# Adding word numbers on TensorE and making the list of neighbour words with five wide VectorE operations

## What is computed

```python
def layer0(X, adj):                       # X 8192x128, adj 8192x8192
    mask = adj != 0
    vals = max over j of (X[j, :] where mask[i, j])      # for each row i
    return where(any(mask, axis=1), vals, 0)

x = layernorm(x + layer0(x, adj))
x = layernorm(x + L1(x, W1, a1, adj))     # thresholded attention
x = layernorm(x + L2(adj, x, W2, a2))     # attention
x = layernorm(x + L3(x, adj, W3, a3))     # attention
```

## Time and profile before

| | us |
|---|---|
| timed, median of 3 | 4908.3 |
| profiled execution, span from first to last instruction | 5439.8 |
| neighbour maximum in the profile, about | 0 to 2222 |
| three attention layers in the profile, about | 2222 to 5440 |

### The profile page before, as it was taken

The page is one execution under the profiler, slowest core; times in us unless marked ns, Lnnn a source line. Parts: engine busy times, 40 slices in busy tenths (PEclk is TensorE's granted clock), DMA queues, the critical chain, the costliest instruction groups (busy, mean ns, idle before and its releaser), DMA issues. The chain is left out here.

```text
span 5439.8 us, 68010 instructions
## 1 busy us (share of the span) xinstructions
PE 4559.6 (84%) x22263; PEld 2172.7 (40%) x22263; DVE 4311.2 (79%) x7371; ACT 2207.6 (41%) x2430; POOL 1205.9 (22%) x1342
## 2 busy tenths in 40 slices
PE   4766776677667766579999999999999999999999
PEld 3333333333333333323443333454444445444444
DVE  6666676667666667788888888889999987999998
ACT  3444444444444444398888888410000001000000
POOL 5555445454444455200000000000000000000000
PEclk6888888888888889889999999999999999999999
DMA  7555555555555555233232332122222202212220
GB/s 272 195 187 184 192 197 185 187 182 194 186 179 188 193 169 166 95 130 122 105 126 111 113 127 105 64 102 83 75 84 79 81 9 99 102 70 98 76 96 14
DMA packets 181695, 709.72 MB, mean 130 GB/s; under 512 B 31168, under 2 KB 39872, under 8 KB 132224
## 3 DMA queue, kind: packets, MB, share of 16 engines
q1 hardware_dynamic: 110816, 566.01, 29.3%
q0 software_dynamic: 33760, 73.21, 4.2%
q10 hardware_dynamic: 36864, 67.13, 3.5%
HBM read 630.59 MB, written 79.82 MB: 131 GB/s over the span
## 5 line engine op out<-in xcount | busy, mean ns | idle before, releaser
L1750 PE MATMUL bank<-w,GX 128*128 128x512 f32 x4096 | 1768.4, 593 | 4.8 <-DVE w L1865 4.8
L1865 DVE SCALAR_TENSOR_TENSOR w<-q,E,m 128x512 f32<-128x512 f32 x2048 | 1472.1, 758 | 130.8 <-PE bank L1750 39.1
L356 POOL DMA_INDIRECT ring<-x_ext,idx x1051 | 1032.8, 983 | 1074.2 <-DVE X L619 316.8
L1750 PEld LDWEIGHTS bank<-w,GX 128*128 128x128 f32 x4096 | 777.7, 191 | 975.3 <-issue 975.2
L607 DVE TENSOR_TENSOR top<-top,sums 128x1024 f32<-128x1024 f32 x484 | 589.2, 1217 | 626.7 <-remote 364.8
L507 PE MATMUL sums<-lone,xs 128*128 128x512 fp8e4 x3000 | 838.3, 421 | 287.0 <-DVE top L607 214.9
L1200 PE MATMUL acc<-w,GX 128*128 128x512 f32 x2048 | 939.6, 605 | 65.8 <-DVE w L1458 62.6
L430 ACT ACTIVATE stage<-tp 128x1024 fp8e4<-128x1024 uint16 x512 | 523.7, 1025 | 1088.1 <-remote 598.3
L1458 DVE SCALAR_TENSOR_TENSOR w<-q,E,u 128x1024 f32<-128x1024 f32 x512 | 634.7, 1274 | 1.9 <-PE acc L1200 1.8
L507 PEld LDWEIGHTS sums<-lone,xs 128*128 128x128 bf16 x3000 | 291.5, 105 | 814.7 <-issue 607.4
L1200 PEld LDWEIGHTS acc<-w,GX 128*128 128x128 f32 x2048 | 371.9, 190 | 564.5 <-issue 413.5
(11 more groups left out here) (250 smaller groups left out, 2919.3 us busy)
## 6 DMA issues: line engine op xcount, KB each, us to landing
adjb<-in_adj SPq DMA_DIRECT2D x256, 1024.0 KB
m<-mask_t SPq DMA_DIRECT2D x128, 1024.0 KB, 4.8
mask_t<-stage ACTq DMA_DIRECT2D x256, 256.0 KB
den_m<-mask_t SPq DMA_DIRECT2D x64, 1024.0 KB, 6.9
keep_m<-mask_t SPq DMA_DIRECT2D x64, 1024.0 KB, 4.9
ring<-x_ext,idx POOLq DMA_INDIRECT x1051
z<-row_scores SPq DMA_DIRECT2D x30, 256.0 KB, 4.6
xt_rows<-XT SPq DMA_DIRECT2D x8, 512.0 KB, 4.7
```

The lines of the kernel that those rows point to most:

```text
L356: pool.indirect_dma_start(ring[:, s, :], None, x_ext, bass.IndirectOffsetOnAxis(ap=idx[:, k, s:s + 1], axis=0)).then_inc(done, 16)
L1750: last = nc.tensor.matmul(acc[b][:, :], GX[:, j, :], w[:, j % WR, :], start=(j == 0), stop=(j == T - 1))
L1865: nc.vector.scalar_tensor_tensor(out=w[:, j % WR, :], in0=q, scalar=E[:, j:j + 1], in1=m[:, b, j, :], op0=ALU.max, op1=ALU.mult).then_inc( ...
```

## The change

TensorE no longer starts the tally with the first count. Before the counts of blocks 0 and 4 one matmul of 512 columns (`one_row` x `numbers`) writes word numbers times 2^-7 into a whole bank of the tally, and the counts add to it. So each code carries its number (0 to 255, within its half of the row) in its lowest bits. `before` is scaled up to 2^20. VectorE then makes: the exponents of the codes (one source, no mask), codes less exponents, the number put into the exponents of words that don't open a group, and the minimum of these with `before`, by which words without an earlier one drop out. That minimum now signals `cnt_used`. The largest eight are taken of each half of `codes`, so `many` has 16 entries; the peeled ones take the places of the 64 words that open a group in `keys`. ScalarE's mask is gone. New constants are made at the start, for which TensorE waits.

```diff
-MORE = 8
+LEAST = 2.0
+HALVES = 2
+HW = NW // HALVES
+NUMBER = 2.0 ** -7
+BEFORE = 2.0 ** 20
+MORE = 8 * HALVES
...
-                if 1 <= t <= T:
-                    act.wait_ge(counted, t)
-                    nc.scalar.activation(opens[:, :, 1:WPG], before, ACT.Relu, bias=top_bit[:, 0:1], scale=-TOP_BIT).then_inc(opens_made, 1)
...
+            word_steps.did(nc.gpsimd.iota(half_no[:, :, :], pattern=[[HW, HALVES], [0, 8]], base=0, channel_multiplier=0))
+            word_steps.do(nc.gpsimd.memset(one_row_f, 0.0))
+            word_steps.do(nc.gpsimd.affine_select(out=one_row_f, in_=one_row_f, compare_op=ALU.not_equal, fill=1.0, base=0, pattern=[[0, P]], channel_multiplier=1))
...
             pe.wait_ge(again, 5)
+            pe.wait_ge(numbers_made, 1)
...
             def count(q, k, e):
 
+                if e % (T // TRB // HALVES) == 0:
+                    bank = slice(e * TRB, e * TRB + T // HALVES)
+                    nc.tensor.matmul(tally[:, bank, :].rearrange("p t c -> p (t c)"), one_row[:, :], numbers[:, :, :].rearrange("p t c -> p (t c)"),
+                                     start=True, stop=False, skip_group_check=True)
                 for g in range(e * TRB, (e + 1) * TRB):
-                    last = nc.tensor.matmul(tally[:, g, :], stage[:, q, g, k * P:(k + 1) * P], powers[:, :], start=True, stop=True)
+                    last = nc.tensor.matmul(tally[:, g, :], stage[:, q, g, k * P:(k + 1) * P], powers[:, :], start=False, stop=True, skip_group_check=True)
...
-                    hold(dve, opens_made, s + 1)
-                    steps.did(nc.vector.tensor_tensor(out=bits(by_group(high)), in0=bits(code_ps), in1=bits(opens[:, :, :]), op=ALU.bitwise_and))
+                    steps.did(nc.vector.tensor_scalar(bits(keys[:, :, :]), bits(code_ps), EXPONENT, None, ALU.bitwise_and))
...
-                    nc.vector.tensor_tensor(out=by_group(x), in0=code_ps, in1=by_group(high), op=ALU.subtract).then_inc(cnt_used, 1)
+                    steps.did(nc.vector.tensor_tensor(out=by_group(x), in0=code_ps, in1=keys[:, :, :], op=ALU.subtract))
+                    steps.settle()
+                    side.did(nc.vector.tensor_tensor(out=bits(not_opening), in0=bits(not_opening), in1=by_group(code_no[:, :])[:, :, 1:WPG], op=ALU.bitwise_or))
                 if finishes:
                     into(old, 0, 2).then_inc(lower_free, 1)
                 if extracts:
-                    hold(dve, cnt_used, s + 2)
-                    steps.do(nc.vector.tensor_scalar(bits(high), bits(x), EXPONENT, None, ALU.bitwise_and))
-                    steps.did(nc.vector.tensor_tensor(out=x, in0=x, in1=high, op=ALU.subtract))
+                    steps.settle()
+                    side.settle()
+                    nc.vector.tensor_tensor(out=not_opening, in0=not_opening, in1=before, op=ALU.min).then_inc(cnt_used, 1)
                 step(2)
                 if extracts:
-                    steps.settle()
-                    steps.did(nc.vector.tensor_tensor(out=bits(x), in0=bits(x), in1=code_no[:, :], op=ALU.bitwise_or))
-                    side.did(nc.vector.tensor_tensor(out=bits(high), in0=bits(high), in1=code_no[:, :], op=ALU.bitwise_or))
-                    steps.settle()
-                    steps.did(nc.vector.max(out=y, in_=x))
+                    for a in range(HALVES):
+                        steps.did(nc.vector.max(out=y[:, 8 * a:8 * a + 8], in_=x[:, a * HW:(a + 1) * HW]))
                 step(3)
...
-                    later = keys[:, NW:NW + (DEEP - 1) * MORE].rearrange("p (d n) -> p d n", n=MORE)
+                    later = keys[:, :, 0].rearrange("p (d n) -> p d n", n=MORE)
...
-                    s.do(nc.gpsimd.memset(earlier[:, :], 1.0))
+                    s.do(nc.gpsimd.memset(earlier[:, :], BEFORE))
```

More of the change, by code:

```diff
@@ L411, in _ @@
             act.sem_inc(evacuated, 2)
-            act.wait_ge(opens_free, 1)
             def lone_pair(p, b):
@@ L663, in phase @@
                 h = HALF
-                tops = tops and quad is not None and k == 0
+                turned = turned and quad is not None and k == 0
                 def bits(ap):
@@ L722, in phase @@
                     steps.settle()
-                    steps.did(nc.vector.tensor_scalar(many_no[:, :], bits(y), NW - 1, None, ALU.bitwise_and))
+                    steps.did(nc.vector.tensor_scalar(many_i[:, :], y, 1.0 / NUMBER, None, ALU.mult))
                 if finishes:
@@ L750, in phase @@
                 if extracts:
-                    later = keys[:, NW:NW + (DEEP - 1) * MORE].rearrange("p (d n) -> p d n", n=MORE)
-                    steps.did(nc.vector.tensor_tensor(out=bits(later), in0=bits(many_high[:, :, :]), in1=many_no[:, :].unsqueeze(1).to_broadcast([P, DEEP - 1, MORE]), op=ALU.bitwise_or))
+                    later = keys[:, :, 0].rearrange("p (d n) -> p d n", n=MORE)
+                    steps.did(nc.vector.tensor_tensor(out=bits(later), in0=bits(many_high[:, :, :]), in1=many_no[:, :].unsqueeze(1).to_broadcast([P, T // MORE, MORE]), op=ALU.bitwise_or))
+                    hold(dve, cnt_used, s + 2)
                     side.settle()
                     steps.settle()
-                    steps.did(nc.vector.max(out=srt[:, 0:8], in_=keys[:, :]))
+                    steps.did(nc.vector.max(out=srt[:, 0:8], in_=listed))
                 step(5)
```

50 lines of the change are left out of this document (29 added, 21 removed).

## The result

The changed kernel takes 4928.9 us, the median of four runs (4926.7 to 4932.8), against 4908.1 us before (median of four, 4901.2 to 4910.6): ratio 1.0047, 95% interval 1.0033 to 1.0061. It is slower by 20.8 us. The prediction was 4930.

The account below looks back on a forecast made before the run. No engine was taken as full: TensorE and VectorE take turns on one `sums` buffer. 60 tiles x (0.29 + 0.05) = 20 us on 4908.3 gave 4928, called 4930 with something for the start; range 4902 to 4950.

Parts of the forecast that it names:

- The reading of what bounds the kernel: Each of a tile's eight steps lasts the longer of a 2.85 us round trip and VectorE's own work; pauses: profiler's.
- 25.0 a tile: Steady tile without pauses: 33.3 us profiled less 8.3 of pauses, taken as near 24.2 plus merging every fourth tile.
- the 24.2: Sum in us of the eight steps of a tile, taken from undisturbed steps in the first profile.
- Step 7, nothing saved: The one-source mask of exponents on PSUM stays 0.60 us; dropping ScalarE's mask saves 0.
- Steps 1 to 3, TensorE handed the tally late: The minimum signals at 3.20 instead of 1.82, with a 0.215 matmul queued behind; step 3 opens later, +0.29 us a tile.
- by the 0.15 from L607's end to the sums: Delay taken from the minimum's end at 3.20 to TensorE going on at 3.35, in us after step 1's maximum.
- Step 4, "+0.05": VectorE-full step: small operations on more `many` entries and 64 later keys add 0.05 us a tile.
- Steps 5 to 7, hidden: Steps 5 to 7 unchanged; step 5's second wide matmul takes TensorE to 2.60 us, under the 2.85 round trip.
- The start: New GpSimd and VectorE operations before the first turn, 1 to 1.5 us in all, taken as 0, upper end 1.5.
- TensorE not late: Rival, chance 0.17: the wait ends before counts are due or slack hides it; 4906 us, within 0.2%.
- VectorE's work setting the time: Rival, chance 0.08: all VectorE savings count, 61 us over 60 tiles, giving 4847 us.
- The spread to step 4: Rival, 0.12 together with dearest bounds: late ScalarE pushes step 4 by up to another 0.3 us a tile; 4947 us.

Follow-up runs that it names:

- b_again: The kernel before, unchanged, profiled a second time: span 4903.2 us without pauses, 4904.9 us timed.
- e8: Changed kernel with only the small operation that makes `need` written with two sources: 4930.43 us, ratio 1.0051.
- e9: Kernel before with only the small operation that makes `need` written with two sources: 4894.03 us, ratio 0.998.
- e1: Changed kernel with the minimum, which signals `cnt_used`, put ahead of the bitwise-or: 4906.79 us, ratio 1.0011.
- e3: Changed kernel without the two 512-column word-number matmuls, the counts starting the tally: 4914.42 us, ratio 1.0025.
- e10: Kernel before with `cnt_used` signalled by L712 instead of L706 and an overwritten 512-column matmul before the counts of blocks 0 and 4: 4923.92 us, ratio 1.0039.
- e4: Changed kernel with the list of 64 later keys (L767) made a second time, into a contiguous tile: 4930.93 us, single run.
- e2: Changed kernel with both 256-element maxima of step 2 done twice, the second pair into an unread tile: 4928.17 us, ratio 1.0054.
- e7: Kernel of e5 with three short VectorE operations moved from steps 7 and 1 into step 0, and `need` written with two sources: 4852.78 us, ratio 0.9897.
- e11: Kernel of e7 with VectorE adding the turned maxima to X ahead of the sums' COPY in every fourth tile: 4834.43 us, ratio 0.9863.
- e5: Kernel of e1 with the peeling of `many` started in step 2 and moved a step earlier, out of step 4: 4890.93 us, ratio 0.9975.

## Why the prediction was right, step by step

**The reading of what bounds the kernel** held. Steps last the longer of the round trip and VectorE's own work (2.85 to within 0.01 in steps 5 and 6, and in step 0 outside every fourth tile). That the pauses are not the kernel's, on which the whole sum rested, is what b_again and the profile after show. The "25.0 a tile" came near the measured 25.28 by two slips that partly cancel: the stretch of 2000 us holds 59 tiles and not 60 (33.9 each), and the pauses lie in fewer than 64 tiles (34.0 a tile over the 60 measured ones, less 25.28, is 8.7 and not 8.3). What the 24.2 lacks is in step 0 (+0.57: the longer first step of every fourth tile, 0.2 of it by the clock's falls), in step 7 (+0.40: the merging, 0.17 of MEMSET waits, and two single steps of 7.0 and 6.7 us) and in step 1 (+0.08). All this is in the tiles of before and of after, so that the difference was not touched much.

**Step 7, nothing saved**: right as to the mask, L701 takes 684 ns as L716 did (683). The rule of the Trainium skill (VectorE: DVE Perf Modes, the perf-mode tier table) that the prediction weighed, up to twice the rate for this operation on PSUM, is not borne out: at twice the rate it would be, as an estimate, some 0.34. ScalarE's mask was indeed free. Step 7 as a whole fell by 0.08, which I did not predict. With the MEMSET waits taken out of both kernels (e8, e9) it is 3.65 and 3.67, so most of the 0.08 is what `need` happened to wait: over 0.25 us in 24 tiles after and in 21 before, but mostly 0.47 us long after and 0.57 before.

**Steps 1 to 3, TensorE handed the tally late**: the mechanism is shown from three sides. Signal earlier: step 2 is 2.85 (e1). No matmul: 2.92 (e3). Both burdens on the old kernel: 3.13 (e10). The term was too large: +0.29 for steps 1 and 2 together, and they came to +0.25 (0.055 and 0.198). The chain in the rows: minimum's end at 3.21 (predicted 3.20); weight load at 3.27, where the prediction had TensorE go on at 3.35; counts at 3.50 (3.565); sums at 4.78 (4.85); step 3 at 6.28 (6.33). The step that failed is the single one "by the 0.15 from L607's end to the sums". From the minimum's end to the load it is 0.06, and in e10 0.05 to the matmul; the 0.15 belongs to the maximum and sums, and was carried to another pair without a row. The 0.215 for the matmul (0.23 between load and counts, 0.22 by e3), the 16 counts, turn and firsts hold to 0.03. In step 1, +0.05 was measured for the +0.03 taken.

**Step 4, "+0.05"**: the mechanism was right (small operations in a step where VectorE is full), the size was not: +0.12. L767 with 64 elements was priced by element count at 219, and the row says 268, 0.05 more, because of where it writes (e4). The remaining 0.02 I did not trace.

**Steps 5 to 7, hidden**: right, 2.84 and 2.86 in both kernels.

**The start**: taken as 0, and it is 0 as far as can be seen. The first maximum starts at 101.3 us in the changed kernel and at 101.4 in b_again.

**The sum**: 0.34 x 60 = 20 was predicted; measured are 0.346 x 60 = 20.8. That it came out closer than its terms is luck: steps 1 and 2 too large by 2 us, step 4 too small by 4, and step 7 with -5 and steps 0 and 3 with +3 not in it at all.

**The rivals.** TensorE not late fell, as the idle time before L494 shows: 69.3 us in 61 waits put down to the minimum. VectorE's work setting the time fell by e2, where 40 us more of it cost nothing. The spread to step 4 fell too: step 3 is 2.86. What I had not seen as a rival, and what moved the profiles of e8 and e10 by 6 and 8 us, as much as the whole term of step 4, are the clock's falls in every fourth tile, 1.0 to 1.7 us each. The changed kernel has them in 10 of 14 tiles and b_again in 9; had it had them in 14 or in 4, its time would have been some 6 to 9 us off my sum. That the range would have held that was luck of its width.

## What to carry to other kernels

Work taken off an engine counts only up to the next arrival it waits for; count it from the first to the next operation that both engines share, in order of time, and not by its share of the span. When an edit moves the last reader of a buffer, follow the signal first: here a signal 1.4 us later and a 0.2 us matmul behind it outweighed 1.1 us of saved VectorE work, and putting one operation ahead of another (e1) took nearly all of it back. Then look for what has to wait although it is short, and for an engine that stands and comes back at its lower clock: the edits of e7 and e11, which went for these two, were worth 38 us of the 68 that the last version gains. Of the 38, some 13 are the waits of `need` and some 16 are fewer falls of the clock; 8 of these 16 came with e7, whose edit gives no reason for them.

## What the runs showed of the hardware

**The one-source form of `need` on VectorE waits until GpSimd's MEMSET has ended, the two-source form does not.** `need`, three elements, took 0.16 us or, with a MEMSET beside it, up to 1.6 us, and then ended 0.03 us after the MEMSET; as a two-source operation it takes 0.154 to 0.181 with as many MEMSETs beside it (e7, 22 of 64). The Trainium skill (SBUF — State Buffer, Who interferes with whom) has a one-source operation between two SBUF operands able to enter a mode that takes the port pair which VectorE shares with GpSimd, so that one of the two blocks; with that rule these runs agree, as far as the waiting goes. They show it for an operation of three elements, which is no faster undisturbed as a one-source operation (0.156 us at the least) than with two sources (0.156 on average). Other one-source operations were not tried.

**TensorE's clock fell in some of the tiles in which it had stood for 2.4 to 2.7 us, and in none of the 14 in which it had stood for 1.25.** With 2.64 to 2.74 us of standing the clock was at 1.2 GHz in the step behind it in 9 of 14 tiles of b_again, 10 of after, 13 of e8, 6 of e9. In e7, where it stood for 2.39, it fell in 6 of 14. Over the twelve profiles without pauses other than e11's it is 112 of 168 tiles; in e11's it is 0 of 14. What decides between two tiles with the same standing is open; nothing in the rows around them differs that I could name. It may be why single executions of one kernel lie up to 20 us apart (e5: 4881.9 to 4901.4), but no run tested that, and e11's four, without any fall in its profile, still lie 6.6 us apart. The Trainium skill (TensorE: Matmul & The Clock Gate, HAM oscillation — how this bites in real kernels) tells of waits between bursts of matmuls after which each burst starts at the lower clock. The rows of 1012.80 and 1015.40 agree in part: the clock falls behind a wait, but only about 1 us into the work that follows (1.00 up to 1016.40, 0.50 from 1016.90), and in other tiles with the same wait it does not fall.

**Writing with a step of 8 words** costs 0.8 ns an element more than writing in a row (269 against 219 ns for 64 elements, e4).

**Pauses that are not the program's** came and went between profiled executions of one kernel: 531.5 us of them in the profile of before, none in b_again. A profile whose span is well above its timed median should be taken again before it is summed.
